# Attention and trigonometric FFN block on one core: who drains the late score banks beside ScalarE's table loads

## What is computed

```python
def kernel_func(q, k):
    scores = jnp.einsum('bhqd,bhkd->bhqk', q, k) / jnp.sqrt(jnp.asarray(HD, q.dtype))
    w = jax.nn.relu(scores)
    return w / (jnp.sum(w, axis=-1, keepdims=True) + KERN_EPS)
...
out = out @ w_out + b_out
y = x + out
mu = jnp.mean(y, axis=-1, keepdims=True)
var = jnp.var(y, axis=-1, keepdims=True)
return (y - mu) * jax.lax.rsqrt(var + LN_EPS) * gamma + beta
...
real = jnp.einsum('bti,io->bto', x, jnp.cos(theta + theta_noise))
imag = jnp.einsum('bti,io->bto', x, jnp.sin(phi + phi_noise))
return jnp.sqrt(real * real + imag * imag)
...
x = x + _L0_attn_ref(_layernorm(x, axis=-1), ...)
x = x + _L0_ffn_ref(_layernorm(x, axis=-1), ...)
```

## Time and profile before

| | |
|---|---|
| median of 3 runs | 426.1 us (425.95 to 426.21) |
| the profiled execution's own time | 425.92 us |
| span in its trace | 424.1 us |
| PE busy | 413.5 us, 97% of the span |
| DVE busy | 330.9 us, 78% |
| ACT busy | 339.3 us, 80% |
| granted TensorE clock | full in all 40 slices of the span |
| score matmuls, line 1051 | 134.0 us busy, x1024 |
| value matmuls, line 1086 | 272.3 us busy, x2048 |

### The profile page before, as it was taken

How to read it: one execution, slowest core, us unless ns; L and a number is a source line. 1 busy time by engine, 2 the same in 40 slices (tenths; PEclk the granted TensorE clock), 3 DMA queues, 4 the chain that set the end, 5 groups by cost and what they waited for, 6 DMA issues and landing times.

```text
span 424.1 us, 8977 instructions
## 1 busy us (share of the span) xinstructions
PE 413.5 (97%) x3270; PEld 120.9 (29%) x3270; DVE 330.9 (78%) x652; ACT 339.3 (80%) x595; POOL 48.3 (11%) x62
## 2 busy tenths in 40 slices
PE   8899999999999999999999999999999999999995
PEld 6323222222222322222222322222222322222234
DVE  6775788777779798867788798767788798777956
ACT  2867878888788888889888888879888798888864
POOL 4793000000000100000400100000100100000111
PEclk9999999999999999999999999999999999999999
DMA  5127841001012100101011100101011000000200
GB/s 167 26 51 144 165 115 41 12 4 47 2 50 58 26 26 8 44 2 51 26 50 57 26 27 0 51 2 51 27 49 56 4 26 0 26 2 27 66 3 25
DMA packets 11133, 17.40 MB, mean 41 GB/s; under 512 B 3092, under 2 KB 4756, under 8 KB 10708
## 3 DMA queue, kind: packets, MB, share of 16 engines
q1 hardware_dynamic: 10948, 16.70, 14.6%
q10 hardware_dynamic: 144, 0.13, 0.1%
HBM read 3.86 MB, written 5.10 MB: 21 GB/s over the span
## 4 chain that ended last, share of the span: by engine, by line
PE 93%; DVE 2%; ACT 2%; DMA 1%; POOL 0%; issue 0%; DVEq 0%
PE pv L1086 60%; PE sc L1051 27%; PE pv L1141 2%; PE pv L983 1%; PE pv L992 1%; PE pv L1004 1%; PE pv L1112 1%; DMA x_sb<-x_dram 1%; ACT w_buf L573 0%; PE pv L1093 0%; DVE stats L683 0%; ACT w_buf L570 0%; PE sc L1141 0%; PE pv L972 0%; ACT L585 0%
## 5 line engine op out<-in xcount | busy, mean ns | idle before, releaser
L1086 PE MATMUL pv<-w_buf,v_sb 128*32 128x512 f32 x2048 | 272.3, 604 | 0.0
L729 DVE TENSOR_SCALAR w_buf<-sc 128x512 f32<-128x512 f32 x256 | 177.0, 691 | 73.2 <-PE sc L1051 63.3
L570 ACT ACTIVATE w_buf<-sc 128x512 f32<-128x512 f32 x256 | 153.1, 598 | 67.1 <-PE sc L1051 66.5
L573 ACT ACTIVATE w_buf<-sc 128x512 f32<-128x512 f32 (+1 forms) x256 | 183.6, 717 | 0.0
L1051 PE MATMUL sc<-q_rep,k_rep 32*128 32x512 f32 x1024 | 134.0, 494 | 2.3 <-ACT w_buf L570 0.9
L733 DVE TENSOR_SCALAR w_buf<-sc 128x512 f32<-128x512 f32 x182 | 123.9, 681 | 1.3 <-PE sc L1051 1.3
L1051 PEld LDWEIGHTS sc<-q_rep,k_rep 32*128 32x128 f32 x1024 | 52.4, 181 | 216.6 <-ACT w_buf L570 175.9
L1086 PEld LDWEIGHTS pv<-w_buf,v_sb 128*32 128x32 f32 x2048 | 40.4, 108 | 66.5 <-ACT w_buf L573 34.9
L468 POOL TENSOR_TENSOR oT<-o_raw,o_scale 128x512 f32<-128x512 f32 (+1 forms) x4 | 5.1, 1280 | 162.6 <-DMA o_scale<-inverse_dram 101.9
L484 POOL TENSOR_TENSOR mag<-sq 128x256 f32<-128x256 f32 x6 | 4.4, 731 | 77.5 <-ACT sq L608 77.5
L474 POOL TENSOR_TENSOR x<-x,mv 128x512 f32<-128x512 f32 (+1 forms) x5 | 4.3, 870 | 68.1 <-DVE x L825 55.5
(11 more groups left out here) (123 smaller groups left out, 148.0 us busy)
## 6 DMA issues: line engine op xcount, KB each, us to landing
pv_dram<-pv_sb SPq DMA_DIRECT2D x15, 256.0 KB, 2.0
q_rep<-q_hi SPq DMA_DIRECT2D x30, 64.0 KB, 2.1
q_rep<-q_lo SPq DMA_DIRECT2D x30, 64.0 KB, 2.1
k_rep<-k_hi SPq DMA_DIRECT2D x6, 256.0 KB, 4.1
k_rep<-k_lo SPq DMA_DIRECT2D x6, 256.0 KB, 5.4
x_sb<-x_dram SPq DMA_DIRECT2D x3, 256.0 KB, 3.9
o_raw<-pv_dram SPq DMA_DIRECT2D x3, 256.0 KB
o_scale<-inverse_dram SPq DMA_DIRECT2D x3, 256.0 KB
```

The costliest lines, as they stand in the source:

```text
L570: nc.scalar.activation(w_buf[:, s % W_STEPS, 0, :], early[:, 0, :], ACT.Relu).then_inc(relu[0], 1)
L573: nc.scalar.activation(w_buf[:, s % W_STEPS, 2:2 + n, :], late[:, 0:n, :], ACT.Relu).then_inc(relu[0], 1)
L729: nc.vector.tensor_scalar(w_buf[:, s % W_STEPS, 1, :], early[:, 1, :], 0.0, None, ALU.max).then_inc(relu[1], 2 if both else 1)
L1086: last = nc.tensor.matmul(bank[32 * i:32 * i + 32, :], v_sb[:, k, HPG * g + i, :], w_buf[:, s % W_STEPS, i, :], start=(k == 0), stop=(k == ...
```

## The change

- The lists of the first pass: in group 2 ACT's both-late steps are (2,3), (2,5), (2,8), (2,10) instead of (2,0), (2,3), (2,8), (2,12); in group 3 they are (3,5), (3,8), (3,11), (3,13) instead of (3,3), (3,8), (3,11), (3,13).
- At (2,12) and (3,3) DVE takes both late banks in one operation of 128x1024, and ACT only its early bank, with an increment of 2.
- At (2,12) ACT runs a sine of one column into a spare tile (sine_table), ahead of the true sine, which moves to (2,14).
- The seven angle pieces stand behind (1,10), (1,12), (1,14), (2,3), (2,5), (2,7) and (2,10).

```diff
-FIRST_BOTH_LATE = ((1, 11, 13, 15), (3, 8, 10, 12, 14), (0, 3, 8, 12), (3, 8, 11, 13))
+FIRST_BOTH_LATE = ((1, 11, 13, 15), (3, 8, 10, 12, 14), (3, 5, 8, 10), (5, 8, 11, 13))
+DVE_BOTH_LATE = ((), (), (12,), (3,))
...
+        def dve_takes_both(c, s):
+
+            return c == 0 and s % NT in DVE_BOTH_LATE[s // NT]
...
-                    nc.scalar.activation(w_buf[:, s % W_STEPS, 0, :], early[:, 0, :], ACT.Relu).then_inc(relu[0], 1)
+                    none = dve_takes_both(c, s)
+                    nc.scalar.activation(w_buf[:, s % W_STEPS, 0, :], early[:, 0, :],
+                                         ACT.Relu).then_inc(relu[0], 2 if none else 1)
+                    if none:
+                        return
...
+                def sine_table():
+
+                    act.wait_ge(angles_ready, 1)
+                    nc.scalar.activation(spare_act[:, :], angles[:, 0, 0:1], ACT.Sin)
...
-                             ((3, 8), lambda: take_q(3)), ((2, 12), trig), ((3, 3), sqrt_table)])
+                             ((3, 8), lambda: take_q(3)), ((2, 12), sine_table), ((2, 14), trig), ((3, 3), sqrt_table)])
...
-                        nc.vector.tensor_scalar(w_buf[:, s % W_STEPS, 3, :], late[:, 1, :],
+                        n = 0 if dve_takes_both(c, s) else 1
+                        nc.vector.tensor_scalar(w_buf[:, s % W_STEPS, 2 + n:4, :], late[:, n:2, :],
...
-                         + [((1 + n // 8, 9 + n % 8 if n < 7 else n - 7), part)
-                            for n, part in enumerate(trig_angles(trig))])
+                         + list(zip(((1, 10), (1, 12), (1, 14), (2, 3), (2, 5), (2, 7), (2, 10)),
+                                    trig_angles(trig))))
```

## The result

| | before | after |
|---|---|---|
| median | 426.06 us (4 runs, 425.95 to 426.21) | 423.50 us (4 runs, 423.44 to 423.51) |
| span of the profiled execution | 424.1 us | 421.6 us |
| PE busy | 413.5 us | 412.7 us |
| DVE busy | 330.9 us | 331.6 us |
| ACT busy | 339.3 us | 338.6 us |

The ratio of the medians is 0.994, its 95% interval 0.9928 to 0.9953; 423.5 us was forecast. The busy times hardly moved: the 2.5 us of the span are time in which PE ran its steps too slowly, and the page's busy shares don't show that. The list of PE's waits shows a part of it: in the stretch of the earlier trace rows it had two rows, 1.6 us, and after it has none, though two cut steps remain. A second pair is the two score matmuls of a step's late half; it is late by what its row lasts over a plain row of 0.50 or 0.51.

What follows compares the result with a forecast made beforehand. TensorE bounds the kernel, so ACT and DVE matter only where PE stands still or runs late; gains 1.05 + 0.82 + 0.72 = 2.59 us take 426.1 to 423.5 us, range 422.7 to 424.6.

Steps and rivals of the forecast that it cites:

- Part 1: Sine load at (2,12): second pair of (2,14) only 0.37 us late, step loses 0.39 instead of 1.44, gain 1.05.
- part 2: Root's table load at (3,3): second pair 0.38 us late, loss 0.40 instead of 1.22, gain 0.82.
- the 0.07 for the increment: At the loads, ACT's early relu with an increment by 2 starts 0.07 us later.
- Part 3: Both-late steps moved to (2,5), (2,10), (3,5): each fits a step, DVE's early 0.07 later within 0.08; cost 0.
- Part 4: Seven angle pieces from (1,10) to (2,10): hidden behind DVE's early-only steps or project_q, gain 0.72 us.
- The 0.07 behind take_q: Score rows of (1,10) and (2,10): 0.07 us lost after take_q, not from the angles.
- The cover of the seventh piece by project_q: Piece at (2,7) makes early(2,8) 0.3 us late, covered by project_q's extra 1.06; uncovered it would cost 0.22.
- (a): Rival: the angle pieces keep their price, the 0.72 us gain is gone, 424.2 us; chance 0.09.
- (b): Rival: DVE is the bound at both loads, wide operation 1.6 us, pairs 0.60 late, 424.0 us; chance 0.06.
- (c): Rival: the sine loads its table again at (2,14), +0.8 us, 424.3 us; chance 0.04.
- (d): Rival: a table switch also costs a drain as long as the load, 1.28 us; 426.1 us, no change; chance 0.05.
- (e): Rival: slower; DVE's wide two-bank PSUM read decides from 2.67 us, at 3.2 us gives 427.2 us; chance 0.03.

Runs made afterwards that it cites:

- the lengthened DVE work: Changed kernel with one more 128x512 DVE read of a late bank ahead of each of its two wide operations; 424.34 us against 423.50.
- the plain-step experiment: Changed kernel without ACT's both-late steps (1,10), (1,12), (1,14), so the first three angle pieces follow plain DVE steps; 423.95 us against 423.43.
- the angles alone: Kernel before with only the angle pieces moved, ACT keeping both late banks and table loads at (2,12), (3,3); 425.36 us, 0.67 under the kernel before.
- the sine ahead: Angle pieces moved and sine table loaded ahead at (2,12), ACT still taking both late banks; 425.06 us, 0.30 under the same without loading ahead.

## Why the prediction was right

**The bound and the place to look.** It held that ACT and DVE cost time only where a second pair is late. All 2.5 us of the span come from the steps named: from the trace of after, (2,14) gives 2.87 - 1.82 = 1.05, (3,5) 2.65 - 1.81 = 0.84, the angle stretch 12.25 - 11.57 = 0.68; together 2.57, less 0.08 by which (1,8) began later in this execution (56.14 and 56.06), ahead of anything that was changed.

**Part 1 and part 2.** Forecast: second pairs 0.37 and 0.38 late, gains 1.05 and 0.82. Measured 0.38 at both, gains 1.05 and 0.84. Each link stood up: the 0.07 for the increment (0.06), the load 0.02 behind the relu's end (0.01 to 0.02), 1.40 from load to next relu (1.41 and 1.40). The wide DVE row was 1.22, between the bounds of 1.10 and 1.36, near the 1.20 taken from DVE's growth with size; the growth of ACT's rows would have been too small. That ACT and not DVE ends the stall was a matter of 0.17 us in the prediction (90.76 against 90.93), and the lengthened DVE work confirmed it: 0.61 more cost 0.46, so the margin is 0.15.

**Part 3.** Right in size, but not quite 0: behind the separate waits the rows are 0.52 and 0.53 long, second pairs 0.01 to 0.02 late. The reason is the term of 0.13 from the end of DVE's relu to PE. Read again from the earlier trace rows it is 0.15: early(1,10) ended at 61.62, and the second pair of (1,11) began at 61.48 + 0.79 - 0.50 = 61.77. The limit is then 0.06 and not 0.08, and the separate wait of 0.06 to 0.07 just reaches it. With 0.60 in place of 0.62, the earlies of the plain-step experiment, 0.69 and 0.94 behind their score rows, should be 0.09 and 0.34 late, and they are 0.09 and 0.35.

**Part 4.** Forecast 0.72, measured 0.68; the term was 0.04 too large, for the reason just given (a few hundredths in eight steps). The 0.07 behind take_q stayed, as said (1.51 from (1,10) to (1,11)). The cover of the seventh piece by project_q held: 82.74 - 80.25 = 2.49, as before. What I had also mis-sized is what the pieces hold DVE for, 0.06 to 0.09 too long each; it did no harm while they were hidden, and made the expectation for the plain steps too large (0.85 for 0.52). The sum is nearer than its terms, 2.59 against 2.57: the 0.02 of part 2 and the 0.04 of this part go opposite ways.

**The rivals.** (a), the angles keeping their price: refuted by the angles alone, 0.67 us. (b), DVE the bound: refuted by the wide row and by the lengthened work. (c), a second load: there is none at (2,14). (Its reason said ten steps of relus without a load; from (2,13) to (3,3) there were seven. In the changed kernel four relus stand between the stand-in and the true sine.) (d), a switch that costs more than its load row: the load starts 0.01 behind the relu's end at 88.30 and the next activation 0.02 behind the load. It is the same, 0.01 to 0.02 on both sides, at the two loads amid the relus in all ten kernels; nothing like a drain of the load's own length is seen. (e) asked for a wide row over 2.67 us; it is 1.22.

## What to carry to other kernels

Where one engine is full and others feed it through a few buffers, don't count an activity's duration but its deadline: from the step's distance, the drain's length and the release time comes how late a drain may start. Here that is 1.43 + 0.01 - 0.69 - 0.15 - 0.54 = 0.06 us for DVE and 1.43 + 0.01 - 0.60 - 0.05 - 0.54 = 0.25 for ACT (step, first pair to second, relu, release, plain start behind the score row). What was later cost what it was over, to within 0.02 in the steps read. Then a fixed cost such as a table load (1.40 us of ACT) belongs beside the step in which the full engine has other work of its own (project_q, 1.06 us): there it was free once DVE took the late banks, while the hand-over in a plain step brought the stall only from 1.44 and 1.22 down to 0.38. Look at the start-to-start distance of the full engine's rows, not at its waits or busy share: the list of waits had 1.6 us of a loss of 3.4, and none of the 0.8 that was left at the loads. The same look at the later passes shows more of it, untouched by the change. PE, score rows of (1,7) and (1,9) in the second pass, kernel after:

```profile
152.48 0.72 PE L1066 MATMUL sc<-q_rep,k_rep 32*128 32x512 f32 x4
...
155.55 0.65 PE L1066 MATMUL sc<-q_rep,k_rep 32*128 32x512 f32 x4
```

These second pairs come 0.21 and 0.14 late in each of the three later passes, about 1.1 us in all, before the change and after it, and PE's list of waits between 120 and 405 us is empty in both kernels. No experiment here went after them.

## What was not expected of the hardware

A relu whose increment is 2 starts 0.06 us later than the same relu with an increment of 1 (0.60 against 0.54 behind its score row), and the wait then is an instruction of its own in the trace. I had read it off one pair of rows; moving one of the two increments to another instruction took it away. The wait list can name the wrong engine: with the sine ahead it gave 0.73 us to DVE, where ACT's relu ended 0.05 us before PE went on. The 0.7 us of DVE in the earlier trace rows is the same case, at (3,5): DVE had drained early(3,4) at 101.81, ACT at 103.20, and PE went on at 103.25.
